# First context and values' weights loaded from ScalarE's queue, low parts shared with VectorE, one wait moved in the last stage

## What is computed

```python
x = x + xattn(layernorm(x), ctx)      # 8 heads of 64: q = x@Wq, k = ctx@Wk, v = ctx@Wv,
                                      # softmax(q k^T / 8) v, then @Wo + bo
x = x + ffn(layernorm(x))             # a shared expert and 8 routed ones (128 -> 256 -> 128, exact gelu),
                                      # weighted by the two highest router probabilities
```

## Time and profile before

| | us |
|---|---|
| runs (3): median, lowest, highest | 405.89, 405.79, 415.48 |
| the profiled execution: whole time | 405.86 |
| the profiled execution: span of the core | 404.1 |
| TensorE busy in the span | 395.5 (98%) |
| VectorE, ScalarE, GpSimd busy | 283.1, 248.0, 238.0 |
| granted clock of TensorE, mean | 1.00 |

### The profile page before, as it was taken

One profiled execution on the slowest core, in us unless ns is written; L12 is line 12 of the kernel. 1 busy time (PEld: TensorE's weight loads), 2 busy tenths in 40 slices (PEclk: granted clock), 3 DMA queues, 4 the chain that ended last, 5 costly groups with the idle time before them and its releaser, 6 DMA issues.

```text
span 404.1 us, 9723 instructions
## 1 busy us (share of the span) xinstructions
PE 395.5 (98%) x3718; PEld 330.4 (82%) x3718; DVE 283.1 (70%) x580; ACT 248.0 (61%) x400; POOL 238.0 (59%) x167
## 2 busy tenths in 40 slices
PE   8999999999999999999999999999999999999996
PEld 6787879797878887979789878888797877887886
DVE  3977898787646868878448687874586857567544
ACT  5678556382864654728837365468281945889782
POOL 6428568786902876447208782645074773588881
PEclk9999999999999999999999999999999999999999
DMA  6700002000000020000000220000000003203400
GB/s 190 202 1 2 2 2 63 2 2 3 0 2 2 3 62 3 2 2 0 3 2 3 63 58 2 0 2 2 2 3 0 2 3 113 98 0 91 146 1 28
DMA packets 17141, 11.77 MB, mean 29 GB/s; under 512 B 10188, under 2 KB 14136, under 8 KB 17096
## 3 DMA queue, kind: packets, MB, share of 16 engines
q1 hardware_dynamic: 17096, 11.15, 10.4%
HBM read 10.55 MB, written 0.56 MB: 27 GB/s over the span
## 4 chain that ended last, share of the span: by engine, by line
PE 85%; ACT 4%; issue 4%; POOL 4%; DVE 3%; DMA 1%; SPq 0%; DVEq 0%; ACTq 0%; POOLq 0%
PE ps L1197 21%; PE ps L1181 16%; PE ps L1028 9%; PE ps L1030 9%; PE ps L1029 9%; PE ps L1122 8%; PE ps L1172 6%; PE ps L1068 2%; PE ps L1129 2%; PE ps L1060 2%; ACT probs L802 1%; POOL kq_lo L704 1%; POOL work L486 1%; DMA raw<-in_ctx_T_dram 1%; ACT xn L725 1%
## 5 line engine op out<-in xcount | busy, mean ns | idle before, releaser
L923 DVE TENSOR_REDUCE maxes<-ps 128x1 f32<-128x402 f32 x256 | 132.6, 570 | 14.5 <-PE ps L1122 9.5
L802 ACT ACTIVATE probs<-ps 128x1024 f32<-128x1024 f32 (+1 forms) x112 | 105.5, 962 | 29.1 <-PE ps L1181 26.0
L486 POOL TENSOR_TENSOR work<-work,probs 128x1024 f32<-128x1024 f32 x45 | 107.4, 2386 | 3.5
L484 POOL TENSOR_TENSOR work<-probs 128x1024 f32<-128x1024 f32 x15 | 36.0, 2398 | 105.1 <-issue 89.4
L1197 PE MATMUL ps<-probs,v_sb 128*64 128x256 f32 (+1 forms) x832 | 93.4, 381 | 0.4 <-DVE work L866 0.4
L1197 PEld LDWEIGHTS ps<-probs,v_sb 128*64 128x64 f32 (+1 forms) x832 | 59.2, 137 | 30.7 <-issue 3.4
L1181 PE MATMUL ps<-kq_hi,kq_lo 64*128 64x256 f32 (+1 forms) x416 | 69.9, 280 | 0.0
L1181 PE MATMUL ps<-kq_lo,kq_hi 64*128 64x256 f32 (+1 forms) x416 | 69.9, 279 | 0.0
L1181 PE MATMUL ps<-kq_hi 64*128 64x256 f32 (+1 forms) x416 | 69.7, 279 | 0.0
L758 ACT COPY repeated<-rden 128x256 f32<-128x256 f32 x16 | 6.5, 405 | 90.0 <-DVE rden L902 90.0
L1122 PE MATMUL ps<-kq_hi 64*128 64x402 f32 x256 | 60.1, 366 | 0.1
(11 more groups left out here) (153 smaller groups left out, 694.5 us busy)
## 6 DMA issues: line engine op xcount, KB each, us to landing
v_sb<-weight_rows SPq DMA_DIRECT2D x12, 256.0 KB, 4.2
raw<-in_ctx_T_dram SPq DMA_DIRECT2D x3, 600.4 KB, 5.0
work<-in_L_ffn_rw_dram SPq DMA_DIRECT2D x1, 1024.0 KB, 7.7
shift_rows<-neg_row SPq DMA_DIRECT2D x64, 0.5 KB, 2.0
raw<-weight_rows SPq DMA_DIRECT2D x4, 256.0 KB, 3.5
raw<-in_ctx_T_dram SPq DMA_DIRECT2D x3, 150.8 KB, 2.8
x_sb<-in_x_dram SPq DMA_DIRECT2D x1, 384.0 KB, 6.6
wo_sb<-in_L_xattn_Wo_dram SPq DMA_DIRECT2D x1, 256.0 KB, 7.0
```

What stands on the lines that cost most here:

```text
L486: ops.tensor_tensor(acc, acc, pr, ALU.add).then_inc(summed, 1)
L802: nc.scalar.activation(dst, src, ACT.Exp, scale=SCALE).then_inc(probs_ready, 1)
L923: v.tensor_reduce(maxes[:, p % 2, i * T + t, blk:blk + 1], src[:, 0:BW], AX.X, ALU.max).then_inc(ring_taken, 1)
```

## The change

Four edits are made.

1. The four loads of context quarters and the load of Wv move from SyncE to ScalarE, where they stand ahead of everything else that this engine does.
2. ScalarE rounds quarter 2 before the transposed x and quarter 3 right after it, ahead of the steps; the `ctx0` step is gone.
3. The low parts of Wv and of context quarter 3 move from GpSimd to VectorE, in the step `wv`, between the queries and key block 1. Wv's low part gets its own semaphore, `wv_split`; `w_split` now counts to 1.
4. In the last stage only part 1 of the second half waits for the copy of the first half's bank.

```diff
-    out = first[:2] + [("wv", 0)] + first[2:3] + [("ctx0", 3)] + pieces[0] + first[3:4] + v0[:2] + pieces[1]
+    out = first[:2] + [("wv", 0)] + first[2:3] + pieces[0] + first[3:4] + v0[:2] + pieces[1]
...
-            load_ctx(0)
-            sp.dma_start(wv_sb, Wv).then_inc(s_wv, 16)
...
-            pool.wait_ge(s_wv, 16)
-            pool.wait_ge(wv_hi_ready, 1)
-            g.tensor_tensor(wv_lo[:], wv_sb, wv_hi[:].bitcast(F32), ALU.subtract).then_inc(w_split, 1)
-            low_part(0, 3)
...
-            pool.wait_ge(w_split, 2)
+            pool.wait_ge(w_split, 1)
...
+            for i in range(BLOCKS):
+                act.dma_start(ctx_raw[:, quarter(i)], ctxT[0][:, quarter(i)]).then_inc(s_ctx0[i], 16)
+            act.dma_start(wv_sb, Wv).then_inc(s_wv, 16)
             act.wait_ge(s_wqk, 32)
             nc.scalar.copy(wk_hi[:, 0:P], wk_sb[:, 0:P]).then_inc(w0_hi_ready, 1)
             nc.scalar.copy(wq_hi[:, 0:P], wq_sb[:, 0:P]).then_inc(w0_hi_ready, 1)
-            for i in range(2):
+            for i in range(3):
                 high_part(0, i)
             act.wait_ge(setup_filled, 1)
             nc.scalar.copy(xnT_hi[:, 0:S], ps[:, 7, 0:S]).then_inc(first_ready, 1)
-            high_part(0, 2)
+            high_part(0, 3)
...
-                elif kind == "ctx0":
-                    high_part(0, w)
...
-                        act.wait_ge(w_split, 1)
+                        act.wait_ge(wv_split, 1)
...
+                if kind == "wv":
+                    dve.wait_ge(s_wv, 16)
+                    dve.wait_ge(wv_hi_ready, 1)
+                    v.tensor_tensor(wv_lo[:], wv_sb, wv_hi[:].bitcast(F32), ALU.subtract).then_inc(wv_split, 1)
+                    dve.wait_ge(ctx_hi_ready, BLOCKS)
+                    dve.wait_ge(ctx_lo_ready, BLOCKS - 1)
+                    cs = quarter(BLOCKS - 1)
+                    v.tensor_tensor(ctxT_lo[:, 0, cs], ctx_raw[:, cs], ctxT_hi[0:C, 0, cs].bitcast(F32), ALU.subtract
+                                    ).then_inc(ctx_lo_ready, 1)
...
-                        pe.wait_ge(w_split, 2)
+                        pe.wait_ge(w_split, 1)
...
                     if c == 0:
-                        pe.wait_ge(w_split, 1)
+                        pe.wait_ge(wv_split, 1)
...
-                        if h:
+                        if part:
 
                             pe.wait_ge(outT_taken, h)
```

More of the change, by code:

```diff
@@ L388, in build @@
         consts_ready = sem("consts_ready")
-        w_split, w1_split = sem("w_split"), sem("w1_split")
+        w_split, wv_split, w1_split = sem("w_split"), sem("wv_split"), sem("w1_split")
         rstd_ready = sem("rstd_ready")
@@ L511, in load_ctx @@
             def load_ctx(b):
[L512 to L517, removed]
+                sp.wait_ge(ctx_lo_ready, BLOCKS * b)
+                sp.dma_start(ctx_raw, ctxT[b]).then_inc(s_ctx[b], 16)
             sp.dma_start(xv[:, 0:1], xd[:, 0:1]).then_inc(s_x0, 16)
```

## The result

| | before | changed |
|---|---|---|
| median of 11 runs each, us | 406.15 | 415.26 |
| lowest, highest, us | 405.25, 415.48 | 407.51, 417.69 |
| ratio of the runs near the fastest of each | | 1.0094, 95% interval 1.0055 to 1.0132 |
| executions with a mean granted clock under 0.99 | | 7 of 12 |
| profiled execution: span, mean clock | 404.1, 1.00 | 415.7, 0.97 |

What follows compares the result with a forecast made beforehand. TensorE, which ends last and has no gap from 10.0 to 25.7 us, was taken to carry any head delay to the end. 405.89 + 0.72 (head: -0.14 + 0.86) - 0.54 (last wait) = 406.07, said as 406.1 us; range 405.4 to 408.3.

Steps and rivals of the forecast that it cites:

- Where the table load goes, and the length of the issues: ScalarE's head: five issues of 0.46 us from 0.72 to 3.02 us, then the table load, Wk rounded at 4.34 us.
- The rival of shared issuing: Head: two queues wait for each other, every issue takes twice as long; 408.4 us; chance 0.27 together with contention.
- When the weights land: Head: ScalarE rounds Wk at 4.34 us instead of 3.60, once ready, Wq 0.21 us later; no later landing counted.
- the term -0.14 of the sum: Head: first quarter rounded at 4.76 us against 4.90, so first keys start at 6.54 us instead of 6.68.
- if x lands 0.3 us later: Head, milder form of shared issuing: transfers contend and queries become late by about as much; 406.4 us.
- VectorE's added work: Between queries and second key block: two added low parts delay the third key block by 0.86 us (0.72 to 0.99).
- Nothing takes it back, all is late by the same amount: After the head: maxima and matmuls shift by +0.72 us, as TensorE has no gap until 25.7 us.
- a wait of about 1 us: Sign in the profile after: TensorE waits this long for VectorE before the third key block, near 10.6 us.
- I gave this 0.02: Chance of slower by two per cent (8.1 us), for a head so long idle that TensorE's clock falls.
- The last wait: Second half, near 379 us: first part's matmuls fill TensorE's wait for the copy; -0.54 us, bounds 0 and 0.66.

Runs made afterwards that it cites:

- e4: Changed kernel with ten instead of three small dummy matmuls between the transposes of x and the first keys; 414.98 us, ratio 1.0146.
- f3: Changed kernel with ten dummy matmuls before the first keys and six before the third key block; 407.85 us, ratio 1.0055.
- f2: e2 with six small dummy matmuls on a free bank before the third key block; 406.69 us.
- e3: Changed kernel with the low parts of Wv and context quarter 3 back on GpSimd; 414.7 us, ratio 1.0035.
- g2: e6 with GpSimd's low parts of the context begun only when VectorE has normalised x; 405.65 us.
- g1: e1 with GpSimd's low parts of the context begun only when VectorE has normalised x; 405.28 us, ratio 0.9992.
- e2: Changed kernel with the four context loads and Wv back on SyncE behind Wq; 414.03 us, ratio 1.0034.
- g3: e1 with only the first context quarter issued by ScalarE; 411.13 us, ratio 1.0019.
- f1: e3 with SyncE also waiting for Wk and Wq to land before issuing any later load; 415.73 us, ratio 1.0025.
- e6: e1 with only the first columns of Wk and Wq issued from ScalarE's queue; 406.48 us, ratio 1.0014.
- e1: Kernel before, with only the last-stage edit (in the second half only part 1 waits for the copy); 405.67 us against 405.51, ratio 1.0004.

## Why the prediction was wrong, point by point

- **Where the table load goes, and the length of the issues**: right. Five issues to 3.05 us, the table to 4.36 us, no rounding possible before. The rival of shared issuing is refuted: 1.85 us for four, with SyncE issuing beside it. The Trainium skill's "Perfetto Trace Analysis", section "DMA Instruction — HWDGE (DVE, Sync)", lets one expect a wait for the lock; if there was one here it did not lengthen any of these issues (0.46 us each with both queues issuing, 0.46 with one).
- **When the weights land**: this step failed. I let Wk be rounded at 4.34 us, as soon as ScalarE was ready, and took it that Wk and Wq land as before. This is the term -0.14 of the sum. I looked at how many microseconds each issue takes and not at what is under way in front of and beside it. Contention had a place in the text only as "if x lands 0.3 us later", a bound that came from no row. It was 0.8 us for x and 2.7 us for Wq, and the first keys moved from 6.68 to 8.54 us instead of to 6.54. The bytes would have told: x, Wk and Wq are 240 KB, and 0.8 MB were put beside them. At the 265 GB/s that the profile shows from 5 to 8 us the latter alone take some 3 us, an estimate of about the size of Wq's lateness; it is no more than that, as Wv, a quarter of these bytes, landed only at 8.5 us, behind Wq. The Trainium skill says it outright: in "DMA: Bandwidth & Descriptors", section "Issuing engines are not separate DMA queues", DMAs of all engines run on the same 16 DMA engines and interleave. The trace agrees (Wq 2.0 us before, 4.7 after, 2.7 with one quarter).
- **VectorE's added work**: right, near the low bound. At full clock 0.99 us lie between the queries' low part and that of the second key block (e4, f3), against 1.12 forecast (0.98 to 1.25), and the third key block is 0.72 and 0.71 us later for it, against +0.86 (+0.72 to +0.99). That f2 as a whole is +0.9 us over before is luck, as other terms are in it.
- **"Nothing takes it back, all is late by the same amount"**: wrong. This step failed too, and it costs the most. I carried both delays on as pure shifts. Here the waits of TensorE were more: behind 1.42, 1.32 and 1.12 us of idling the granted clock went from 1.00 to 0.50, and executions with a low clock are some 7 to 10 us longer than those at full clock (e3: 414.7 to 416.6 against 406.9). I had computed the second gap (0.39 + 0.86 = 1.25 us; measured 1.12) and written down "a wait of about 1 us" as something to look for, without asking what the clock does in it. I gave this 0.02. It decides the median: 415.26 us, where the sum at full clock would have been about 408 (before 405.9, +1.7 for the first keys, +0.7 for VectorE, up to -0.5 at the last wait).
- **The last wait**: the mechanism was right, the size taken from one execution. 0.54 us were counted; 0 to 0.5 are there by the traces, depending on when VectorE's copy ends against TensorE's arrival.

## What to carry to other kernels

A second queue gave earlier issues here, and what was landing at that time paid for it: Wq took 4.7 us instead of 2.0. So ask first what the loads brought forward will meet. Even 112 KB of weights on that queue gained nothing (g2 405.65 us, g1 without them 405.28). Where a step adds a wait to TensorE, ask for its length and not only for its sum: with six small matmuls that nobody reads the median was 406.7 us (f2), without them 414.0 (e2, on another chip). And when an engine's instructions are suddenly several times as long, look for the partner it shares SBUF with before moving work between the two.

## What the runs showed that I had not expected

- The clock fell behind idle stretches of 1.42 us (changed kernel), 1.39 us (g3), 1.32 us (f1) and 1.12 us (e2, e4), and stayed at 1.2 GHz for 16 to 24 us of nearly full work. In the traces in which the longest stretch, once TensorE had begun, was 0.91 us (e6), 0.89 (e3), 0.75 (f2), 0.70 (e1) or 0.62 (f3) it did not. Of all executions it was low in none of 12 of e6, 12 of f2 and 6 of f3, in 2 of 12 of e1 and in 5 of 9 of e3. Why it falls in some executions of a kernel and not in others is not shown; e3 and f1, which differ little, idled 0.89 us in a traced execution at full clock and 1.32 in one at low clock, each with another 0.7 to 0.8 us two microseconds ahead. The kernel before had it low in 4 of 83 with clocks on record, one of these at 0.852 and 432.8 us, and no trace shows what preceded that.
- VectorE's instructions that read SBUF alone waited for GpSimd's low parts: 1.47 us instead of 0.73 and 1.14 instead of 0.28; one with an operand in PSUM did not (0.42 us). The Trainium skill's "SBUF — State Buffer", section "SBUF: two separate sides", describes this as an exclusive lock on a shared pair of ports, held for the whole instruction. The trace agrees: VectorE's two ended 0.1 us behind GpSimd's. It made an earlier load of the first quarter worse than a late one (407.26 us in e1's traced execution, quarter rounded at 4.50 us).
- In e1 and e6 matmuls of 402 columns follow each other at 0.33 us from 7.8 to about 10 us, as they do at a clock of 0.50, while the granted clock is shown as 1.00 in that stretch. The slow pace begins with the transposes of x, behind an idle stretch of 0.70 and 0.91 us. It costs about 1 us, so a part of what e1's traced execution and e6 lose, and g1 saves, is this and not the instructions of VectorE themselves. I can't say why the clock column does not show it.
- Left open: some executions of several kernels took about 10 us longer at a mean clock of 0.998 to 1.00: before (two of 25 at 416.2 us, one of 29 at 415.9), the changed kernel (417.7) and three of 14 of g3. No trace shows one.
